# Joining the route stage and the expert stage of a two-layer transformer kernel, with rotation jobs placed between them

## The reference, cut to what matters

```python
xn = _layernorm(x)
# attention of layer 1
qkv = (xn @ qkv_w.T).reshape(Bb, Ss, 3, H, D)
q = _rope(q, c, s); k = _rope(k, c, s)      # t1*c - t2*s, t1*s + t2*c
attn = softmax(q k^T * SCALE - p*log1p(a*dist))
# gate of layer 1
idx = argmax(softmax(xt @ Wr + br))          # one expert for each row
h = relu(onehot . xn2 . W1 + b1[idx]);  y = (onehot . h . W2 + b2[idx]) * gates
x = x + s * silu(y)
```

## Time and profile before

| | |
|---|---|
| median of 3 runs | 2864.39 us (2864.07 to 2866.3) |
| the profiled execution | 2865.5 us, of which 2863.8 us are its span |
| mean granted TensorE clock | 0.978 of full |
| route stage | from about 1380.0 to 1425.1 us of the span |
| expert and rotation stage | from 1425.1 to about 1581.5 us |

### The profile page before, as it was taken

One profiled execution on the slowest core, in us unless ns is written; L12 is line 12 of the kernel. 1 busy time (PEld: TensorE's weight loads), 2 busy tenths in 40 slices (PEclk: granted clock), 3 DMA queues, 4 the chain that ended last, 5 costly groups with the idle time before them and its releaser, 6 DMA issues. The chain is left out here.

```text
span 2863.8 us, 46679 instructions
## 1 busy us (share of the span) xinstructions
PE 2714.5 (95%) x17528; PEld 1141.7 (40%) x17528; DVE 2460.7 (86%) x3263; ACT 1572.8 (55%) x1970; POOL 2430.1 (85%) x1179
## 2 busy tenths in 40 slices
PE   4899999999999999999589599999999999999998
PEld 3434333433343444443365144434434444443443
DVE  6578888888888888886678699999999999999997
ACT  4345555555555555555255355655555565556554
POOL 0219999999999999999245599999999999999997
PEclk9999999999999999999699699999999999999999
DMA  5441111111111111110323422222223222222201
GB/s 117 144 154 30 30 30 30 31 29 27 27 27 25 27 27 26 30 30 1 96 103 144 142 70 71 65 48 52 69 70 73 73 74 70 73 73 70 74 16 30
DMA packets 77938, 171.82 MB, mean 60 GB/s; under 512 B 21505, under 2 KB 35210, under 8 KB 75538
## 3 DMA queue, kind: packets, MB, share of 16 engines
q1 hardware_dynamic: 67618, 150.21, 18.8%
q0 software_dynamic: 10096, 18.62, 3.5%
HBM read 113.34 MB, written 38.93 MB: 53 GB/s over the span
## 5 line engine op out<-in xcount | busy, mean ns | idle before, releaser
L1004 POOL TENSOR_TENSOR a_sums<-a_sums,room 128x1024 f32<-128x1024 f32 x504 | 1178.8, 2367 | 24.7 <-ACT room L782 24.7
L696 PE MATMUL a_ov<-room,va 128*64 128x512 f32 x4096 | 992.5, 606 | 0.0
L782 ACT ACTIVATE room<-room,sscale 128x1024 f32<-128x1024 f32 x512 | 587.8, 1148 | 457.3 <-DVE room L884 457.1
L852 DVE TENSOR_REDUCE a_mx<-a_jb 128x1 f32<-128x1024 f32 x496 | 606.6, 1223 | 180.3 <-PE a_jb L652 180.0
L1004 POOL TENSOR_TENSOR a_sums<-room 128x1024 f32<-128x1024 f32 x256 | 605.1, 2365 | 70.5 <-ACT room L786 35.7
L847 DVE CUSTOM_DVE_ANT_0 a_junk<-a_jb,a_tab 128x1024 bf16<-128x1024 f32 x501 | 611.0, 1220 | 37.2 <-PE a_jb L652 25.8
L884 DVE TENSOR_TENSOR room<-a_st,a_tab 128x1024 f32<-128x1024 f32 x512 | 623.9, 1220 | 15.4 <-PE a_st L685 15.4
L786 ACT ACTIVATE room<-room,sscale 128x1024 f32<-128x1024 f32 x256 | 294.0, 1148 | 352.0 <-DVE room L871 352.0
L651 PE MATMUL a_jb<-a_kh,a_qh 64*128 64x512 f16 x997 | 383.3, 384 | 8.1 <-DVE a_mx L847 5.9
L685 PE MATMUL a_st<-a_qh,a_kh 64*128 64x512 f16 x2048 | 390.1, 378 | 0.1
L685 PE MATMUL a_st<-a_ql,a_kh 64*128 64x512 f16 x2048 | 389.9, 377 | 0.0
(11 more groups left out here) (241 smaller groups left out, 2552.4 us busy)
## 6 DMA issues: line engine op xcount, KB each, us to landing
a_tab<-bias_line SPq DMA_DIRECT2D x16, 1984.0 KB, 9.6
acc<-a_part POOLq DMA_DIRECT2D x63, 256.0 KB, 3.3
qk_high<-room SPq DMA_DIRECT2D x16, 512.0 KB, 2.6
qk_low<-room SPq DMA_DIRECT2D x16, 512.0 KB, 3.6
a_qh<-qk_high SPq DMA_DIRECT2D x32, 256.0 KB, 4.2
a_kh<-qk_high SPq DMA_DIRECT2D x32, 256.0 KB, 4.9
a_ql<-qk_low SPq DMA_DIRECT2D x32, 256.0 KB, 6.8
a_kl<-qk_low SPq DMA_DIRECT2D x32, 256.0 KB, 7.2
```

The source lines that it names most:

```text
L696: last = nc.tensor.matmul(ov[t * DH:(t + 1) * DH, :], k.va[:, 2 * s + t, h * DH:(h + 1) * DH], prob[:, step % RING, t * QC:(t + 1) * QC], ...
L782: nc.scalar.activation(prob[:, r, :], prob[:, r, :], ACT.Exp, scale=k.sscale[:, layer:layer + 1])\
L852: nc.vector.reduce_max(mx[:, n % 2, j // 2, j % 2:j % 2 + 1], scratch(n, j), AX.X).then_inc(max_done, 1)
L1004: nc.gpsimd.tensor_tensor(a, first, prob[:, step % RING, :], ALU.add).then_inc(summed, 1)
```

## The change

The two stages become one, `middle_stage`, with one `Block`. For that the router's scratch moves into the unused half of `gate`, its PSUM results move into the banks of `dn`, and the early value vectors use the two banks of `up`, half a tile each, in place of four banks of their own. New semaphores `regrouped` and `named` say that the regrouped weights and the owners are there. On PE, `project(0)` follows the early values, the owners are read in two lots of 11 and 12 with `project(1)` between them, and tiles begin in job 2. The last values go three to a job into jobs 14 and 15. POOL's and DVE's rotation work follows their route work in order.

```diff
+            pe.wait_ge(regrouped, 4)
+            project(0)
+            pe.wait_ge(named, 1)
             pe.wait_ge(biases_loaded, 32)
             for j in range(FT):
                 last = nc.tensor.matmul(bt[:, j, :], b1[:, j * P:(j + 1) * P], hot[:, :], start=True, stop=True)
             last.then_inc(spread, 1)
-            project(0)
-            owners = [pe.value_load(tiles[0:1, i:i + 1], min_val=0, max_val=NE - 1) for i in range(TL)]
+            owners = [pe.value_load(tiles[0:1, i:i + 1], min_val=0, max_val=NE - 1) for i in range(TL // 2)]
+            project(1)
+            owners += [pe.value_load(tiles[0:1, i:i + 1], min_val=0, max_val=NE - 1) for i in range(TL // 2, TL)]
             pe.wait_ge(weights_loaded, 16 * (1 + FT))
             for j in range(NJOB):
-                if j >= 1:
+                if j >= 2:
                     project(j)
```

```diff
-        work = [[i for i in range(TL) if 1 + i // 2 == j] for j in range(NJOB)]
-        late = [[q for q in range(NVAL, NT) if NJOB - (NT - q + 1) // 2 == j] for j in range(NJOB)]
+        BEGIN = 2
+        work = [[i for i in range(TL) if BEGIN + i // 2 == j] for j in range(NJOB)]
+        late = [[q for q in range(NVAL, NT) if NJOB - 1 - (NT - 1 - q) // 3 == j] for j in range(NJOB)]
```

```diff
             def values_of(q):
-                if q >= 2:
-                    pe.wait_ge(val_copied, q - 1)
+                if q == NVAL:
+                    pe.wait_ge(relu_done, TL)
                 for c in range(2):
-                    last = nc.tensor.matmul(val[:, q % 2, c * QC:(c + 1) * QC], k.xnT[:, q * P:(q + 1) * P],
-                                            k.w1[:, 2, c * QC:(c + 1) * QC], start=True, stop=True)
-                last.then_inc(valued, 1)
+                    if q >= 1:
+                        pe.wait_ge(val_copied, 2 * (q - 1) + c + 1)
+                    nc.tensor.matmul(flat(up[:, c, :, :]), k.xnT[:, q * P:(q + 1) * P], k.w1[:, 2, c * QC:(c + 1) * QC],
+                                     start=True, stop=True).then_inc(valued, 1)
```

More of the change, by code:

```diff
@@ L1033, in middle_stages @@
         w2 = weights[:, NE * FF:].rearrange("p (j e d) -> p j e d", j=FT, e=NE)
[L1034 to L1041, removed]
+        regrouped, named = m.sem("ex_regrouped"), m.sem("ex_named")
         wr, br = m.sb("rt_w", [D, NE]), m.sb("rt_b", [P, NE])
@@ L1103, in _ @@
                                              k.acc[:, q, :], None).then_inc(scattered, 16)
+            for j in range(NJOB):
+                b = j % 2
+                pool.wait_ge(prod, 4 * j + 2)
+                if j >= 1:
+                    pool.wait_ge(low, 2 * j - 1)
+                nc.gpsimd.tensor_tensor(first[:, b, :], first[:, b, :], product[:, 0, :], ALU.subtract).then_inc(rot, 1)
+                pool.wait_ge(prod, 4 * j + 4)
+                if j >= 1:
+                    pool.wait_ge(low, 2 * j)
+                nc.gpsimd.tensor_tensor(second[:, b, :], second[:, b, :], product[:, 1, :], ALU.add).then_inc(rot, 1)
+            nc.gpsimd.tensor_copy(flat(k.wo[:, :, :]), flat(k.wo1[:, :, :]))
         @block.tensor
@@ L1129, in _, with project @@
                 values_of(q)
+            def project(j):
+                g, i, half = jobs[j]
+                for r, (part, ready) in enumerate(((low_part, a_ready), (high_part, b_ready))):
+                    if j >= 1:
+                        pe.wait_ge(prod, 4 * (j - 1) + 3 + r)
+                    for c in range(2):
+                        q0 = half * 1024 + c * 512
+                        last = nc.tensor.matmul(part[:, c * 512:(c + 1) * 512], wqk[:, i, r, g * P:(g + 1) * P],
+                                                k.xnT[:, q0:q0 + 512], start=True, stop=True)
+                    last.then_inc(ready, 1)
@@ new lines, in downward @@
+            def downward(i):
+                o = dn[:, i % 4, :]
+                if i % 4 == 0 and i >= 4:
+                    pe.wait_ge(y_copied, i // 4)
+                nc.tensor.matmul(o, hot[:, i:i + 1].broadcast_to([NE, P]), b2[:, :], start=True, stop=False)
+                pe.wait_ge(relu_done, i + 1)
+                for j in range(FT):
+                    w = w2[:, j, bass.ds(owners[i], 1), :].rearrange("p a d -> p (a d)")
+                    last = nc.tensor.matmul(o, hT[:, i % 2, j, :], w, start=False, stop=(j == FT - 1))
+                last.then_inc(dn_done, 1)
@@ new lines, in _ @@
+            pe.wait_ge(weights_loaded, 16 * (1 + FT))
+            for j in range(NJOB):
+                if j >= 2:
+                    project(j)
+                for i in work[j]:
+                    if i == 0:
+                        pe.wait_ge(b1_copied, 1)
+                        turn(0)
+                    if i % 4 == 0 and i // 4 + 1 < NG:
+                        turn(i // 4 + 1)
+                    upward(i)
+                    if i >= 1:
+                        downward(i - 1)
+                    if i == TL - 1:
+                        downward(i)
+                for q in late[j]:
+                    values_of(q)
@@ L1395, in pick @@
                                      ACT.Copy).then_inc(picked, 1)
[L1397 to L1401 removed]
+            act.wait_ge(regrouped, 4)
+            act.wait_ge(named, 1)
             pick(0)
```

374 lines of the change are left out of this document (151 added, 223 removed).

## The result

The changed kernel takes **2846.9 us** (2846.4 to 2847.3) where the kernel before takes 2865.5 us (2864.1 to 2867.1) beside it: a ratio of 0.9937 [0.9925, 0.9948], 18.6 us. One run of 3972.5 us, with a granted clock of 0.65, is left out.

What follows compares the result with a forecast made beforehand. PE was taken to bound the jobs with tiles, so that stretch should start earlier with fewer jobs behind it. Terms 6.1 + 6.3 = 12.4 us, from 2864.4 to 2852.0 us; range 2847.5 to 2858.5 us.

Steps and rivals of the forecast that it cites:

- Tiles from job 2: First term: in the joined stage, job 2, the first with tiles, starts at 1434.65 us, 6.1 us earlier.
- The second lot: PE's 12 owner loads behind job 1's matmuls: 8.1 us from 1424.8, ending at 1432.9 and hidden.
- the rows: Sorted rows read back at 1433.0 us, before the transposes at 1440.3, so hidden with 7 us to spare.
- the early values: Early values on half banks: five tiles left after the ranking, ending 1.6 us later at the worst; cost nothing.
- The end: Second term: two jobs instead of three behind the last tile, with three value tiles each; gain 6.3 us.
- both of my estimates: Interval between DVE's first products of the last two jobs: 9.0 us, or 9.7 us if ACT holds PE up.
- The tail: Job 15's third value tile delays ACT's last copy by 1.85 us, hidden by DVE's last operation's 3.38 us wait.
- The scatters: POOL's last four scatters beside DVE's job 0 products: issues still 0.96 us, no price up to about 5 us of delay.
- The rule against which I weighed it: DVE instructions with two SBUF inputs contend with GpSimd reading SBUF; job 0's products, with one, cost the scatters nothing.
- the unknown costs: First term 1.6 to 10.5 us, second 4.05 to 6.6; stayed near the middle, PE probably cooling again before job 2.
- the rival to which I gave 0.13: A quicker clock: it rises during job 1 and stays up into job 2, 2847.3 to 2850 us; chance 0.13.
- The bounds of 5.6 and 17.1 us: Least and greatest total gain from the unknown costs of both terms: 2847.3 to 2858.8 us.

Runs made afterwards that it cites:

- experiment 3: Changed kernel with all 23 owners read in one lot ahead of job 1: 2859.58 us, repeated 2860.25 us.
- experiment 4: Changed kernel with each owner read at its tile, behind that job's matmuls, none ahead: 2846.14 us, repeated 2846.88 us.
- first timing: The changed kernel as first measured, chip not recorded: 2846.9 us against 2865.5 us for the kernel before.
- third timing: The changed kernel unaltered, timed again on chip 1: 2848.84 us, ratio 0.9949 to the kernel before.
- second timing: The changed kernel unaltered, timed again on chip 14: 2854.05 us, ratio 0.9962 to the kernel before.
- fourth timing: The changed kernel unaltered, timed again on chip 14: 2857.43 us, ratio 0.9969 to the kernel before.
- experiment 1: Changed kernel unaltered, three more times: 2854.05, 2848.84 and 2857.43 us; the kernel before against itself: 2864.8 us.
- experiment 2: Changed kernel with tiles from job 1 again and two value tiles in each of the last four jobs: 2856.32 us, repeated 2855.84 us.
- Experiment 8: Changed kernel with five extra matmuls that nobody reads, only between jobs 1 and 2: 2851.93 us beside the changed kernel's 2857.43.

## Why the prediction was right in its terms and missed the number

- **"Tiles from job 2", 6.1 us: right where there is no pause.** From the ledger it is 6.75 us there (23.68 - 16.93), and 4.2 and 3.8 us with the pause. From the owners to job 2 I had 1434.65 - 1417.14 = 17.5 us; the profiles without the pause show 16.93 and 17.02. The loads took 7.6 us against 7.4, job 1's products 5.7 us against 6.4, as the clock rose within it. The second lot was hidden (experiments 3 and 4), the rows were not waited for, and the early values ended in time.
- **"The end", 6.3 us: 6.84 in every profile.** The interval is 8.78 us, below both of my estimates: PE's three value tiles took 5.51 us and ACT did not hold it up. The tail was hidden, 14.06 us behind the last first product against 14.09.
- **The scatters: right.** 958 ns with DVE's products beside them. The rule against which I weighed it, in the Trainium skill, SBUF — State Buffer, "Who interferes with whom", agrees with this row. It agrees at the end of the stage too, where `low_half` has two SBUF inputs and takes 2.60 and 2.73 us beside POOL's sum and copy, against a usual 1.22 us.
- **The step that failed** is the choice at the end of the unknown costs, which put the clock's gain in job 2 at nothing: the clock falls "with 3.5 us of idle PE ahead of job 2, probably again". The gap is 3.67 us, and in the profiles of the first and third timing the clock stayed up; in the second and fourth it fell. Full clock there was worth 2.6 us in the first profile (11.32 - 8.73). It is the rival to which I gave 0.13, and of four profiles it holds in two. I had argued from one profile of before, in which the gap ahead of job 1 was 7.46 us, twice as long, so it was no evidence for this gap.
- **The surplus, term by term.** The first profile is 19.1 us shorter and not 12.4. Of these 6.7 us the clock in job 2 makes 2.6, the first term 0.6, the last 0.5, and the two columns outside the stage 2.9.
- **What the forecast left out** has no row in one profile. The pause in the loads costs 2.3 to 2.9 us and takes the gain the other way. What lies outside the stage moves by 2 to 4 us, and the profile of before had a late start and a slow `a_tab`. So the gain, 7.3 to 18.6 us by timing, has a mean of 13.2 us, near the 12.4, but with the clock and the pause pulling opposite ways, so this nearness is partly luck; three of the four times lie in the range and the first 0.6 us under it. The bounds of 5.6 and 17.1 us held the terms, but I gave the range no width for what two timings of one kernel differ by.

**Open.** What makes the pause behind the 8th load. It is the same load each time. All seven profiles from chip 14 in which the loads stand in a row behind the bias spread have it (experiments 1, 2, 3, 8), and no profile known to be from another chip has it, the same program on chip 1 included. So it may belong to the chip rather than to chance; one profile on chip 1 is too few to tell. The kernel before was no slower on chip 14 (2865.2 and 2864.8 us, against 2864.6 on chips 1 and 9). Within one timing the times can split too: in the third, three of five lie at 2847.4 to 2848.8 us and two at 2851.7 and 2852.0, and only one of the five was profiled. No instructions were being fetched then: of the transfers' queues, from 1417 to 1427 us of the fourth timing's profile, only those of data appear:

```profile
q0 software_dynamic: 212, 0.41, 12.0%
q1 hardware_dynamic: 12, 0.02, 1.7%
```

Open too is whether the pause itself makes the clock's rise late. With two lots the late rise stands in every profile with the pause and in none without it; with one lot (experiment 3) the pause stands with an early rise. Experiment 8 parts their prices, not their causes.

## What to carry to other kernels

A register load costs PE's queue 0.64 to 0.67 us. Behind a full queue of matmuls it is free; ahead of a matmul that others wait for, every one counts. Read late, and with the clock held up, the owners give the best version here: 2845.1 us, some 19.5 us under the kernel before. Joining the two stages was worth nothing by itself here; what was moved across the joint was. A change of ten microseconds wants several timings, on more than one chip, and the stage's own length from each profile: here the stage had one of two lengths, each repeated to 0.4 us, while the timings spread over 10.5 us.

## What the runs showed of the hardware

- The same program has job 2 at full or half clock (8.7 or 11.6 us up to job 3), behind the same 3.67 us of idle time. The clock stayed up where it had risen 4.0 to 4.2 us into job 1 (first and third timing, experiments 3 and 4), and fell where it had risen 5.4 to 5.7 us into it (second and fourth, experiment 2). The Trainium skill, TensorE: Matmul & The Clock Gate, Part 1, ties the clock to how busy PE was recently; both outcomes are compatible with that, and no run here shows what sets the moment of the rise.
- Job 1 starts 7.6 us behind the owners, with eleven register loads between, in two profiles, and 9.4 and 9.7 us behind them in two others of the same program on chip 14, with the excess behind one load. The Trainium skill, DMA: Bandwidth & Descriptors, "Latency and other measured facts", gives a register load a floor of about 600 ns; the pitch here, 0.64 us, agrees, though the load itself takes 0.30 us of it.
- POOL's copy at the end, beside DVE's two operations with two SBUF inputs, takes 2.89 us against 1.89 us before. Nothing waited for it.

```profile
1557.56 2.89 POOL L1187 COPY wo<-wo 128x2048 f32<-128x2048 f32 x1
```
